# A mixture of experts with 47 tiles in place of 48, one-hot rows made by two engines in turns, and the last sums taken by quarters of the tokens

## The reference

```python
h = _rms(x, ff_ln_w)
logits = h @ wg                                   # 16 experts
topv, topi = jax.lax.top_k(logits, 4)
gate = softmax(topv)
weights = zeros_like(logits).at[..., topi].set(gate)
a = silu(einsum('bsd,edh->bseh', h, w1)) * einsum('bsd,edh->bseh', h, w3)
y = einsum('bseh,ehd->bsed', a, w2)
x = x + einsum('bsed,bse->bsd', y, weights)
```

## Time and profile before

| | |
|---|---|
| median of 3 runs | 863.56 us (863.39 to 863.63) |
| the profiled execution, its own time | 863.33 us |
| its span in the trace | 861.5 us |
| PE busy | 634.3 us (74%) |
| DVE busy | 616.5 us (72%) |
| ACT busy | 441.7 us (51%) |
| POOL busy | 445.0 us (52%) |

### The profile page before, as it was taken

The page is one execution under the profiler, slowest core; times in us unless marked ns, Lnnn a source line. Parts: engine busy times, 40 slices in busy tenths (PEclk is TensorE's granted clock), DMA queues, the critical chain, the costliest instruction groups (busy, mean ns, idle before and its releaser), DMA issues.

```text
span 861.5 us, 17134 instructions
## 1 busy us (share of the span) xinstructions
PE 634.3 (74%) x5889; PEld 462.7 (54%) x5889; DVE 616.5 (72%) x1476; ACT 441.7 (51%) x1230; POOL 445.0 (52%) x397
## 2 busy tenths in 40 slices
PE   0214997277878754589988998899798638999980
PEld 0102666255646542378666866776587515666650
DVE  5998758787887787958786777678776393555544
ACT  4712633176857711368336824773486206767650
POOL 1463763189999903435334532553264216777760
PEclk9998998698989967889999999999999758999995
DMA  9400130327656502000000000000300543333437
GB/s 291 160 1 0 50 99 21 102 75 221 206 182 198 184 37 110 1 2 2 2 1 0 0 0 0 0 0 0 146 2 2 222 160 91 108 104 107 108 88 250
DMA packets 39896, 71.73 MB, mean 83 GB/s; under 512 B 5024, under 2 KB 31392, under 8 KB 39328
## 3 DMA queue, kind: packets, MB, share of 16 engines
q1 hardware_dynamic: 35232, 58.03, 20.1%
q0 software_dynamic: 4608, 12.98, 5.1%
HBM read 49.96 MB, written 21.04 MB: 82 GB/s over the span
## 4 chain that ended last, share of the span: by engine, by line
PE 28%; POOL 25%; issue 23%; DVE 16%; DMA 3%; ACT 3%; SPq 1%; POOLq 0%; DVEq 0%; ACTq 0%
POOL arena L706 8%; PE ps L1940 8%; PE ps L1963 4%; PE ps L1648 3%; PE ps L1615 2%; POOL arena L661 2%; POOL arena L657 2%; PE ps L1575 2%; POOL arena L696 2%; PE ps L1593 2%; POOL work L696 2%; DVE xn L1007 1%; PE ps L1917 1%; PE ps L1847 1%; PE ps L1952 1%
## 5 line engine op out<-in xcount | busy, mean ns | idle before, releaser
L706 POOL TENSOR_TENSOR arena<-arena,tiny 128x512 f32<-128x512 f32 x64 | 93.9, 1467 | 99.1 <-DVE tiny L1364 99.1
L922 ACT ACTIVATE arena<-ps,tiny 128x128 f32<-128x128 f32 (+1 forms) x256 | 104.9, 436 | 33.4 <-DVE tiny L1338 33.4
L1338 DVE TENSOR_REDUCE tiny<-ps 128x4 f32<-128x512 f32 x64 | 61.1, 954 | 35.9 <-PE ps L1793 35.5
L1940 PE MATMUL ps<-arena 128*128 (+1 forms) x288 | 72.4, 389 | 0.8 <-issue 0.3
L1791 PE MATMUL ps<-arena 128*128 128x128 f16 (+1 forms) x256 | 61.5, 258 | 14.9 <-ACT arena L922 10.5
L1648 PE MATMUL ps<-arena,xt_hi 128*128 128x512 f16 (+1 forms) x224 | 64.4, 372 | 3.6 <-DVE xt_lo L1137 3.0
L728 POOL DMA_INDIRECT arena<-h_store,arena x48 | 47.0, 980 | 33.6 <-DVE arena L1477 19.3
L1491 DVE SCALAR_TENSOR_TENSOR ps<-ps,arena 128x256 f32<-128x256 f32 x48 | 20.8, 433 | 57.6 <-ACT arena L972 57.6
L1360 DVE COPY arena<-ps 128x512 f32<-128x512 f32 x64 | 44.0, 687 | 23.9 <-PE ps L1832 23.9
L1793 PE MATMUL ps<-arena 128*128 128x128 f16 (+1 forms) x256 | 60.4, 255 | 0.0
L734 POOL DMA_INDIRECT y_store<-arena x48 | 47.4, 988 | 21.4 <-issue 12.2
(11 more groups left out here) (298 smaller groups left out, 1851.5 us busy)
## 6 DMA issues: line engine op xcount, KB each, us to landing
e_store<-arena SPq DMA_DIRECT2D x16, 768.0 KB, 4.3
arena<-e_store SPq DMA_DIRECT2D x16, 768.0 KB, 7.3
xn<-w_dram SPq DMA_DIRECT2D x24, 256.0 KB, 4.6
work<-w_dram SPq DMA_DIRECT2D x24, 256.0 KB, 4.7
arena<-w_gate_up_t_dram SPq DMA_DIRECT2D x2, 1024.0 KB, 9.0
arena<-wq_dram SPq DMA_DIRECT2D x2, 1024.0 KB, 7.5
arena<-wo_dram SPq DMA_DIRECT2D x2, 1024.0 KB, 5.4
work<-y_store SPq DMA_DIRECT2D x4, 512.0 KB, 6.5
```

The source lines that it names most:

```text
L706: nc.gpsimd.tensor_tensor(p, p, arec[:, u % 4, :].unsqueeze(2).broadcast_to([P, GH, L]), ALU.mult)\
L922: nc.scalar.activation(ap_[i % 3][:, h, 0:L], ps[:, (i % 2) * 2 + h // 2, (h % 2) * S:(h % 2) * S + L], ACT.Exp, bias=anm[:, i % 4, h:h + ...
L1338: nc.vector.tensor_reduce(anm[:, i % 4, :].rearrange("p (m h) -> p m h", m=2), scores, AX.X, ALU.max, negate=True).then_inc(a_max, 1)
L1940: last = mm(ps[:, 2 + i % 2, :], xg[:, i % 2, x_half * KB + k, :], weights(hidden_weights(slot, w_half, k), i), start=(n == 0), stop=(n == 5))
```

## The change

There is one tile less (47: 16 first tiles and 31 more; 4096 pairs never need more). `slot_of` is computed before `one_tile`, and `sel_ready` tells GpSimd of it. The even `one_slot` arrays are made by VectorE, the odd ones by GpSimd, and TensorE waits for the two in turns. The last loads, sums and stores go by quarters (256 tokens) with one semaphore for each quarter. The arrays behind `one_tile` in the arena move down by some words, since several are one tile shorter.

```diff
-TILES = NE + TOKENS * TOP_K // P
+TILES = NE + TOKENS * TOP_K // P - 1
...
             for i in range(YBUF):
-                sp.wait_ge(y_sent[i], 16 * TILES // YBUF)
-            for c in range(2):
+                sp.wait_ge(y_sent[i], 16 * len(range(i, TILES, YBUF)))
+            for b in range(B):
                 for i, dst in enumerate(y_back):
-                    rows = y_store[GROUP_AT[i] + c * CHUNK:GROUP_AT[i] + (c + 1) * CHUNK, :]
-                    sp.dma_start(dst[:, c * TC:(c + 1) * TC, :], rows.rearrange("(t p) d -> p t d", p=P))\
-                        .then_inc(fetched[1 + c * 2 + i // 2], 16)
+                    rows = y_store[GROUP_AT[i] + b * S:GROUP_AT[i] + (b + 1) * S, :]
+                    sp.dma_start(dst[:, b * TB:(b + 1) * TB, :], rows.rearrange("(t p) d -> p t d", p=P))\
+                        .then_inc(fetched[1 + b], 16)
             outs = out.rearrange("(t p) d -> p t d", p=P)
-            for c in range(2):
-                ts = slice(c * TC, (c + 1) * TC)
-                sp.wait_ge(total_ready, c + 1)
+            for b in range(B):
+                ts = slice(b * TB, (b + 1) * TB)
+                sp.wait_ge(total_ready, b + 1)
                 sp.dma_start(outs[:, ts, :], x[:, ts, :]).then_inc(stored, 16)
...
+            pool.wait_ge(sel_ready, 2)
+            for t in range(T):
+                for j in range(1, TOP_K, 2):
+                    nc.gpsimd.tensor_scalar(one_slot[:, t * TOP_K + j, :], slot_ids, slot_of[:, t, j:j + 1],
+                                            token_ids[:, t, j:j + 1], ALU.is_equal, ALU.mult).then_inc(const_cast, 1)
...
+            nc.vector.scalar_tensor_tensor(slot_of, tile_of, -float(P), four, ALU.mult, ALU.add).then_inc(sel_ready, 1)
             nc.vector.tensor_tensor(one_tile, tile_ids.unsqueeze(1).broadcast_to(picks),
                                     tile_of.rearrange("p t j -> p (t j)").unsqueeze(2).broadcast_to(picks), ALU.is_equal)\
                 .then_inc(one_tile_ready, 1)
-            link(nc.vector.scalar_tensor_tensor(slot_of, tile_of, -float(P), four, ALU.mult, ALU.add))
+            vec.wait_ge(sel_ready, 2)
             for t in range(T):
-                for j in range(TOP_K):
+                for j in range(0, TOP_K, 2):
                     nc.vector.tensor_scalar(one_slot[:, t * TOP_K + j, :], slot_ids, slot_of[:, t, j:j + 1],
...
-            for c in range(2):
-                ts = slice(c * TC, (c + 1) * TC)
+            for b in range(B):
+                ts = slice(b * TB, (b + 1) * TB)
+                vec.wait_ge(fetched[1 + b], 16 * 3 + 16 * TOP_K)
                 for i, src in enumerate(y_back):
-                    vec.wait_ge(fetched[1 + c * 2 + i // 2], 16 * 3 + 32)
                     last = nc.vector.tensor_tensor(x[:, ts, :], x[:, ts, :], src[:, ts, :], ALU.add)
...
             for i in range(T * TOP_K):
-                pe.wait_ge(one_slot_ready, i + 1)
+                if i % 2:
+                    pe.wait_ge(const_cast, 4 + i // 2 + 1)
+                else:
+                    pe.wait_ge(one_slot_ready, i // 2 + 1)
```

More of the change, by code:

```diff
@@ L236, in build @@
         slot_ids = route[:, 0:64].bitcast(F16)
-        tile_ids = route[:, 64:88].bitcast(F16)
+        tile_ids = route[:, 64:88].bitcast(F16)[:, 0:TILES]
         first_base = route[:, 97:113]
@@ L557, in _ @@
             for i in range(YBUF):
-                sp.wait_ge(y_sent[i], 16 * TILES // YBUF)
-            for c in range(2):
+                sp.wait_ge(y_sent[i], 16 * len(range(i, TILES, YBUF)))
+            for b in range(B):
                 for i, dst in enumerate(y_back):
-                    rows = y_store[GROUP_AT[i] + c * CHUNK:GROUP_AT[i] + (c + 1) * CHUNK, :]
-                    sp.dma_start(dst[:, c * TC:(c + 1) * TC, :], rows.rearrange("(t p) d -> p t d", p=P))\
-                        .then_inc(fetched[1 + c * 2 + i // 2], 16)
+                    rows = y_store[GROUP_AT[i] + b * S:GROUP_AT[i] + (b + 1) * S, :]
+                    sp.dma_start(dst[:, b * TB:(b + 1) * TB, :], rows.rearrange("(t p) d -> p t d", p=P))\
+                        .then_inc(fetched[1 + b], 16)
             outs = out.rearrange("(t p) d -> p t d", p=P)
-            for c in range(2):
-                ts = slice(c * TC, (c + 1) * TC)
-                sp.wait_ge(total_ready, c + 1)
+            for b in range(B):
+                ts = slice(b * TB, (b + 1) * TB)
+                sp.wait_ge(total_ready, b + 1)
                 sp.dma_start(outs[:, ts, :], x[:, ts, :]).then_inc(stored, 16)
-            sp.wait_ge(stored, 32)
+            sp.wait_ge(stored, 16 * B)
         CONSTS = 12 * 16
@@ L2013, in inputs_for @@
     route[:, 0:64] = np.arange(1, P + 1).astype(np.float16).view(np.float32)
-    route[:, 64:88] = np.arange(TILES).astype(np.float16).view(np.float32)
+    route[:, 64:88] = np.arange(TILES + 1).astype(np.float16).view(np.float32)
     token = p[:, None, None] + P * np.arange(T)[None, :, None]
```

## The result

The changed kernel takes 866.39 us (median of 11 runs, 864.68 to 868.46), the kernel before, run beside it, 863.33 us (11 runs, 860.73 to 865.09). The ratio is 1.0040, 95% interval 1.0026 to 1.0054: slower by 0.4%, where about 0.35% faster had been forecast. The profiled execution took 866.49 us (span 864.7; before 861.5).

The account below looks back on a forecast made before the run. VectorE was taken to bound the routing, TensorE and GpSimd together the tile loop, load transfers the end. Terms -2.5 - 0.2 - 0.35 = -3.05 us gave 860.5 us against the median, own range 859.3 to 861.7.

Parts of the forecast that it names:

- A: Tile loop: one tile less takes one round from TensorE and a gather and send from GpSimd, -2.5 us.
- B: Routing: one-hot arrays shared by VectorE and GpSimd, -0.2 us, bounds -2.3 and +2.5.
- Two of them make 0.38, and some 0.03 for a two-step operation gives 0.41 us: Routing: GpSimd's own pitch for an array, priced from a cast and two pointer operations, 0.41 us.
- rival 3: Routing: GpSimd's comparison is a slow operation; at 1.67 us an array +18 us, 881 us in all. Chance 0.06.
- The step ahead of it: Routing: GpSimd waits for `one_tile` to end and finishes its first array near 700.0 us.
- Where both have a queue of short operations they alternate: Routing: short VectorE and GpSimd operations take turns, adding 0.05 us to each GpSimd array, 0.46 us in all.
- Rival 2: Routing: the engines take turns in full, each GpSimd array costing 0.64 us, +2.5 us there, 863.2 us total. Chance 0.12.
- p: Routing: GpSimd's pitch, the time for each one-hot array, taken as 0.46 us.
- C: End of the kernel: last loads, sums and stores by quarters, -0.35 us, bounds -0.75 and +1.5.
- they land at about the times of VectorE's four old starts: End: the 1 MiB load quarters land at about 846.6, 849.6, 852.6 and 855.6 us.

Follow-up runs that it names:

- e2: The kernel before with one tile less (47) and nothing else changed: 860.55 us, ratio 0.9971 to the kernel before.
- e5: The changed kernel with 21 more GpSimd operations (three rounds of seven forms) behind its 8th array, to price them: 880.27 us, one run.
- e6: The changed kernel with `one_tile`'s second input read from PSUM by way of a short VectorE copy: 864.62 us, one run.
- e3: The kernel before with only the last loads, sums and stores by quarters (48 tiles, old routing): 863.67 us, ratio 1.0001 to the kernel before.
- e12: The changed kernel measured again, nothing altered: 866.06 us, ratio 1.0035 to the kernel before.
- e8: The kernel before with 47 tiles, loads by halves, and the last half's third and fourth sums by quarters, each with its store: 859.03 us, ratio 0.9947.
- e10: Against the kernel before: 47 tiles, 8 of 32 arrays on GpSimd, `one_tile` reading its tiles from PSUM, last two sums and stores by quarters: 858.00 us, ratio 0.9939.
- e7: Against the kernel before: 47 tiles, `slot_of` first, 6 of the 32 arrays on GpSimd, the end by halves: 857.91 us, ratio 0.9936.

## Why the prediction was wrong

**A was right.** 47 tiles gave -2.51 us from the first `weigh` to the last, against -2.5; e2 gave 2.5 us by the clock of the whole kernel. GpSimd and TensorE did shrink alike.

**B failed at "Two of them make 0.38, and some 0.03 for a two-step operation gives 0.41 us".** The own pitch is 0.77 us (e5), not 0.41: a comparison costs 0.26 to 0.33 us more than a product. I had priced it from a cast and a product, though rival 3 itself said that "no row has a comparison". Of the 0.36 us missing, the comparison is 0.26. A two-step operation with constants takes 0.38 where the same sum had 0.27, another 0.11, and the two pointers were right (0.13 with products, 0.14 in the sum).

The step ahead of it held: GpSimd's first array did wait for `one_tile` (2.33 us in place of 0.81, e6). It ended at 701.18, or 700.6 with the 0.6 us of the later start taken off, where I had said 700.0; the 0.6 us between are the array's own length, for `one_tile` ended at 700.37, or 699.8 with the same 0.6 taken off, as forecast. With 15 x 0.797 = 11.95 in place of 15 x 0.46 = 6.9 the term becomes -0.2 + 5.05 + 0.6 = +5.5, which is the +5.47 measured.

The step behind it, "Where both have a queue of short operations they alternate", failed too, though that cost little here. VectorE's 16 arrays ended in 3.65 us, 0.228 each, as if alone (0.225 in the earlier trace rows), and about four of them passed in one of GpSimd's. The records of three of the sixteen are 0.13 us longer (434 ns against 304), but the array behind each starts 0.22 us after it, as after all the others, so VectorE paid nothing. GpSimd's took 0.82 to 0.98 us beside VectorE's over all these runs, 0.79 without; in the changed kernel its first four starts behind `one_tile` are 0.81 to 0.89 us apart where the later ones are 0.775, 0.3 us in all. Why isn't shown. Rival 2 was therefore wrong for these operations: neither engine held the other up for its whole instruction. The Trainium skill's rule that a VectorE instruction in a two-port mode and a GpSimd instruction fully block each other ("SBUF — State Buffer", the same section; the prediction left its condition, the two-port mode, out) would have given +2.5 us; nothing of that kind is seen at these arrays, and no run shows in which mode they ran.

**What came true was rival 3**, by its mechanism and by its point of decision: "slower than before by over 0.2%" "when B exceeds +4.6, that is at p = 0.78". The pitch was 0.797, B was +5.47. I gave it 0.06. Of what B took, 0.76 us came back with the earlier rise of the clock, which no step of the prediction had. Two of the prediction's sums are off without bearing on this: at a pitch of 1.67 us rival 3 gives 863.56 - 2.5 + 18 - 0.35 = 878.7 us and not 881, and the upper end of the forecast's own range is 861.9 (860.5 + 0.75 + 0.6) and not 861.7.

**C was off by 0.65 us in the profiled execution: -0.35 forecast, +0.30 in its trace, nothing in the time (e3).** The sums (+0.38, forecast +0.4) and the last store (-0.82, forecast -0.75) came as said. What failed is "they land at about the times of VectorE's four old starts". The first quarter's sums started 6.14 us behind SP's first load, where the first two rows of the first half had been there after 5.54, and from the first load to the start of the last sums that wait for loads it was 15.36 us in place of 14.62. Over the six executions with quarters it was 14.98 to 15.82, over the eight with halves 14.59 to 14.77, so with quarters the last of the data does come in later. Whether that is the size of the loads, their 16 issues or the early stores was not tried. Nor could VectorE make it up, with 2.87 us of sums a quarter. The +0.30 is that of one execution: from SP's first load to the end the six with quarters took 20.42 to 21.25 us (e12, the same kernel again, has the 20.42), and the five with halves throughout 20.50 to 20.66. So the forecast gain of 0.35 us is in none of the six, and a loss is not shown either.

**The sum**: -2.51 + 5.47 - 0.76 + 0.08 + 0.30 = +2.6 us, and with the +0.6 ahead of the change +3.2, the difference of the spans.

## What to carry to other kernels

An operation is priced by its own function as well as by its shape and engine: where the trace has no row of that function on that engine, the upper bound is the slowest row of any function there, and the point at which it decides belongs into the main case, not into a rival of 0.06. Work that is split between two engines is split by their pitches, not by halves: here they are 0.22 and 0.8 to 0.9 us, and GpSimd's first array is held up besides, so 26 to 6 gained 2.5 us where 16 to 16 lost 4.7. Cutting the last transfer shortens what comes behind it: in e8, with the loads by halves as before and only the last two sums and the last store cut, the end is 0.5 us shorter, while with loads, sums and stores by quarters nothing was gained. Which part of the quarters takes the gain back isn't shown.

## What the runs showed of the hardware

- GpSimd (e5, one execution, three rounds): a comparison with a product, 128 elements, two pointers, 0.77 us start to start; two products in its place 0.51; each without pointers 0.71 and 0.38. 16 or 32 bit elements make no difference, and 128 more elements cost 0.43 us, 3.3 ns each. VectorE does the same array in 0.225 us.
- A GpSimd operation that stood beside a VectorE step with two inputs in SBUF took 2.33 us; with one of the two in PSUM it took 0.81 (e6) and 0.82 (e10).
- TensorE's granted clock rose from 0.50 to full 6.4 us behind the first tile's start in the kernel before, 4.4 in the changed one and 3.8 in e7 (714.04, with the first tile at 710.27). Ahead of the tiles TensorE was busy 4.66 us of the 5 from 700 to 705 before, 1.50 after and 4.46 in e7, so the busier stretch ahead doesn't explain the earlier rise, and what does isn't shown.
